# The second product of a feed-forward block turned over: features on partitions, residual and bias on VectorE, transposes after

## What is computed

```python
h = elu(_gat_heads(enc_inputs, adj, W_heads, a_heads))       # 4 heads, [B, N, 4*256]
out = elu(_gat_heads(h, adj, W_out[None], a_out[None])[:, 0]) # [B, N, 256]
ffn = jnp.maximum(out @ w1 + b1, 0.0) @ w2 + b2
y = ffn + out
mu, var = y.mean(-1, keepdims=True), y.var(-1, keepdims=True)
L1 = (y - mu) / jnp.sqrt(var + 1e-5) * ln_gamma + ln_beta
# the result is x1 + L1, with x1 the output of the first layer
```

## Time and profile before

| | |
|---|---|
| time, median of 3 runs | 1722.63 us (1721.34 to 1722.68) |
| span of the profiled execution | 1722.6 us |
| its own time beside the span | the same; nothing lies around the span |
| PE / weight loads busy | 1584.4 us (92%) / 1319.3 us (77%) |
| VectorE busy | 1452.3 us (84%) |
| ScalarE busy | 1382.1 us (80%) |
| GpSimd busy | 1004.7 us (58%) |
| mean granted clock of TensorE | 0.975 of full speed |

### The profile page before, as it was taken

The page is one execution under the profiler, slowest core; times in us unless marked ns, Lnnn a source line. Parts: engine busy times, 40 slices in busy tenths (PEclk is TensorE's granted clock), DMA queues, the critical chain, the costliest instruction groups (busy, mean ns, idle before and its releaser), DMA issues.

```text
span 1722.6 us, 36184 instructions
## 1 busy us (share of the span) xinstructions
PE 1584.4 (92%) x13119; PEld 1319.3 (77%) x13120; DVE 1452.3 (84%) x2520; ACT 1382.1 (80%) x1858; POOL 1004.7 (58%) x1425
## 2 busy tenths in 40 slices
PE   5548999999999999999999999999999999999965
PEld 3336878788787887788887887888777888888854
DVE  5877699879998899979999799988999798898583
ACT  4177499879988799878997799878997799999660
POOL 4064367447575566656575566656666475675271
PEclk9769999999999999999999999999999999999988
DMA  8266499749986698678977699868976698798572
GB/s 262 57 147 115 94 190 162 120 95 189 174 151 117 123 187 164 118 122 160 189 141 117 113 184 178 137 98 152 190 156 112 104 172 172 129 133 147 101 118 36
DMA packets 780882, 242.45 MB, mean 141 GB/s; under 512 B 746368, under 2 KB 774016, under 8 KB 780576
## 3 DMA queue, kind: packets, MB, share of 16 engines
q1 hardware_dynamic: 771744, 231.70, 72.1%
q0 software_dynamic: 8960, 8.42, 4.3%
HBM read 38.54 MB, written 16.94 MB: 32 GB/s over the span
## 4 chain that ended last, share of the span: by engine, by line
PE 49%; DVE 18%; ACT 13%; issue 10%; DMA 5%; POOL 3%; SPq 1%; DVEq 0%; ACTq 0%; POOLq 0%
PE ps L129 11%; PE ps L1260 7%; PE ps L1261 7%; PE ps L1266 7%; DVE p_lo L1041 5%; PE ps L138 5%; PE ps L1280 4%; PE ps L1293 3%; ACT p_hi L925 3%; ACT xr L912 3%; DVE xr L1034 3%; PE ps L1341 2%; DMA cat<-f_rows 2%; ACT xr L918 2%; DVE ht_lo L1066 2%
## 5 line engine op out<-in xcount | busy, mean ns | idle before, releaser
L1260 PE MATMUL ps<-pt_hi,hv_hi 128*128 128x256 f16 x2048 | 463.8, 274 | 26.4 <-DMA pt_hi<-p_hi 26.4
L1261 PE MATMUL ps<-pt_hi,hv_lo 128*128 128x256 f16 x2048 | 463.7, 274 | 0.0
L1041 DVE SCALAR_TENSOR_TENSOR p_lo<-xr,rden,p_hi 128x1024 f16<-128x1024 f32 x320 | 409.6, 1280 | 30.4 <-ACT p_hi L925 30.4
L925 ACT ACTIVATE p_hi<-xr,rden 128x1024 f16<-128x1024 f32 x320 | 365.4, 1142 | 32.8 <-POOL rden L849 32.8
L847 POOL TENSOR_SCALAR den<-sums 128x1 f32<-128x1 f32 x320 | 156.4, 489 | 363.2 <-ACT xr L918 361.2
L918 ACT ACTIVATE xr<-xr,shift 128x1024 f32<-128x1024 f32 x320 | 365.5, 1142 | 2.4 <-POOL shift L862 2.4
L1034 DVE CUSTOM_DVE_ANT_0 xr<-cat,mask_add 128x1024 f32<-128x1024 f32 x256 | 311.2, 1217 | 7.5 <-DMA cat<-f_rows 7.5
L912 ACT ACTIVATE xr<-xr,f1h 128x1024 f32<-128x1024 f32 x256 | 292.6, 1143 | 5.5 <-DVE mx L1034 5.5
L849 POOL TENSOR_TENSOR rden<-den,minus_one 128x1 f32<-128x1 f32 x320 | 268.3, 838 | 26.7
L860 POOL TENSOR_SCALAR zt<-mx,f1h 128x1 f32<-128x1 f32 x256 | 197.6, 772 | 120.0 <-DVE mx L1034 117.1
L1266 PE MATMUL ps<-pt_lo,hv_hi 128*128 128x256 f16 x2048 | 266.3, 273 | 0.9 <-DMA pt_lo<-p_lo 0.9
(11 more groups left out here) (192 smaller groups left out, 3193.3 us busy)
## 6 DMA issues: line engine op xcount, KB each, us to landing
cat<-f_rows SPq DMA_DIRECT2D x32, 512.0 KB, 4.6
out<-xx SPq DMA_DIRECT2D x32, 256.0 KB, 2.4
xx<-in_x SPq DMA_DIRECT2D x28, 256.0 KB, 3.3
out<-fin POOLq DMA_DIRECT2D x28, 256.0 KB, 5.3
pt_hi<-p_hi SPq DMA_TRANSPOSE x320, 3.3
pt_lo<-p_lo SPq DMA_TRANSPOSE x320, 3.3
adj_i<-in_adj SPq DMA_DIRECT2D x4, 1024.0 KB, 11.7
f2o<-f2o_rows SPq DMA_DIRECT2D x8, 512.0 KB, 4.4
```

Of the source, the lines that this page charges most:

```text
L925: nc.scalar.activation(p_hi[:, k % P_SLOTS, :], xr[:, k % X_SLOTS, :], ACT.Copy, scale=rden[:, k % 8:k % 8 + 1]).then_inc(hi_done, 1)
L1041: nc.vector.scalar_tensor_tensor(p_lo[:, k % P_SLOTS, :], xr[:, k % X_SLOTS, :], rden[:, k % 8:k % 8 + 1], p_hi[:, k % P_SLOTS, :], ALU.mu ...
L1260: nc.tensor.matmul(to, vh, hi, start=t == 0, stop=False)
L1261: nc.tensor.matmul(to, vl, hi, start=False, stop=False)
```

## The change

`ff2` now keeps features on partitions, like `ff1`: for each of two blocks of output features, w2 is the stationary operand and 512 tokens stream. The identity products are gone. `y_out` adds bias (a column now, `b2_col`) and residual on VectorE and writes into o2T in place. A new PE task, `turn_y`, turns the eight 128 by 128 blocks over with f32 transposes into psB. A new VectorE task, `norm_y`, takes stats and means from psB and does the gain from there, right away; only the gain (`lny_gain`) frees psB. The due steps of the FFN are set anew, and those of m0 to m3 with mj_high and mj_low (but not mj_low3) are one later in `STEADY`.

```diff
-        FFN = ("ff1_0", "ff2_0", "ff1_1", "ff2_1")
+        FFN = ("ff1_0", "ff2_0", "turn_y0", "ff1_1", "ff2_1", "turn_y1")
-        STEADY: m0=-31, m1=-30, m2=-29, m3=-28, mj_high0=-31, mj_high1=-29, mj_high2=-28, mj_high3=-27, mj_low0=-30, mj_low1=-29, mj_low2=-28, mj_low3=-25
+        STEADY: m0=-30, m1=-29, m2=-28, m3=-27, mj_high0=-30, mj_high1=-28, mj_high2=-27, mj_high3=-26, mj_low0=-29, mj_low1=-28, mj_low2=-27, mj_low3=-25
-        CLOSING = dict(ff1_0=-1, ff2_0=2, ff1_1=4, ff2_1=6, hidden_0=1, hidden_1=5, y_0=4, y_1=9, save_f2o=-22, load_f2o=-16)
-        LAST = dict(ff1_0=3, ff2_0=3, ff1_1=5, ff2_1=7, hidden_0=2, hidden_1=5, y_0=4, y_1=8, save_f2o=-13, load_f2o=-12)
+        CLOSING = dict(ff1_0=-1, hidden_0=0, ff2_0=1, y_0=2, turn_y0=3, norm_0=4, rstd_0=5, rescale_0=6, add_0=7,
+                       ff1_1=5, hidden_1=6, ff2_1=6, y_1=7, turn_y1=8, norm_1=9, rstd_1=10, rescale_1=11, add_1=12, save_f2o=-22, load_f2o=-16)
+        LAST = dict(ff1_0=3, hidden_0=3, ff2_0=3, y_0=4, turn_y0=4, norm_0=5, rstd_0=5, rescale_0=6, add_0=7,
+                    ff1_1=5, hidden_1=6, ff2_1=7, y_1=8, turn_y1=8, norm_1=9, rstd_1=9, rescale_1=10, add_1=11, save_f2o=-13, load_f2o=-12)
...
-            if name[:2] == "ff":
-                return (ff_done if name[:3] == "ff1" else y_done), 2 * s + i + 1
+            if name in FFN:
+                return {"ff1": ff_done, "ff2": y_done, "tur": lny_gain}[name[:3]], 2 * s + i + 1
...
             def y_out(p, i):
-                y = y_of(p, i).rearrange("p (t f) -> p t f", f=F)
-                nc.vector.tensor_tensor(y, general(which)[:, :].rearrange("p (t f) -> p t f", f=F), b2_bc[:, :].unsqueeze(1).to_broadcast([P, half, F]), ALU.add).then_inc(y_done, 1)
-                hold(dve, "dve", y_done, 2 * p + i + 1)
+                for m in range(KF):
+                    part = o2T_of(p, i)[:, m, :]
+                    last = nc.vector.scalar_tensor_tensor(part, general(which)[:, m * 512:(m + 1) * 512], b2_col[:, m:m + 1], part, ALU.add, ALU.add)
+                last.then_inc(y_done, 1)
+
+            def norm_y(p, i):
+                which, seq = bank(f"turn_y{i}", p)
+                dve.wait_ge(bank_full[which], seq + 1)
+                turned = general(which)[:, :].rearrange("p (t f) -> p t f", f=F)
+                if 2 * p + i:
+                    dve.wait_ge(lny_done, 2 * p + i)
                 for t in range(half):
-                    last = nc.vector.bn_stats(stats_y[:, t, :], y[:, t, :])
+                    last = nc.vector.bn_stats(stats_y[:, t, :], turned[:, t, :])
...
                 if 2 * p + i:
-                    hold(dve, "dve", lny_gain, 2 * p + i)
                     hold(dve, "dve", lny_pow, 2 * p + i)
...
-            def gain(p, i):
                 dve.wait_ge(lny_mv, 2 * p + i + 1)
                 for t in range(half):
-                    part = y_of(p, i)[:, t * F:(t + 1) * F]
-                    last = nc.vector.scalar_tensor_tensor(part, part, mv_y[:, t, 0:1], gamma_bc[:, :], ALU.subtract, ALU.mult)
+                    last = nc.vector.scalar_tensor_tensor(y_of(p, i)[:, t * F:(t + 1) * F], turned[:, t, :], mv_y[:, t, 0:1], gamma_bc[:, :], ALU.subtract, ALU.mult)
                 last.then_inc(lny_gain, 1)
...
             def ff2(p, i):
-                for t in range(half):
-                    tok = slice(t * P, (t + 1) * P)
-                    for k in range(KF):
-                        nc.tensor.matmul(to[:, t * F:(t + 1) * F], ff_half[:, k * 512 + t * P:k * 512 + (t + 1) * P], w2_sb[:, k, :], start=k == 0, stop=False)
-                    for k in range(KF):
-                        last = nc.tensor.matmul(to[:, t * F + k * P:t * F + (k + 1) * P], o2T_of(p, i)[:, k, tok], ident[:, :], start=False, stop=k == KF - 1)
+                for m in range(KF):
+                    last = product(to[:, m * 512:(m + 1) * 512], [(w2_sb[:, k, m * P:(m + 1) * P], ff_half[:, k * 512:(k + 1) * 512]) for k in range(KF)])
                 last.then_inc(full, 1)
+
+            def turn_y(p, i):
+                to, full = open_bank(f"turn_y{i}", p)
+                pe.wait_ge(y_done, 2 * p + i + 1)
+                for t in range(half):
+                    for k in range(KF):
+                        last = nc.tensor.transpose(to[:, t * F + k * P:t * F + (k + 1) * P], o2T_of(p, i)[:, k, t * P:(t + 1) * P], ident[:, :])
+                last.then_inc(full, 1)
```

More of the change, by code:

```diff
@@ L70, in build @@
         b1_col = sb("b1_col", [P, KF], F32)
-        b2_bc = sb("b2_bc", [P, F], F32)
+        b2_col = sb("b2_col", [P, KF], F32)
         gamma_bc = sb("gamma_bc", [P, F], F32)
@@ L251, in _ @@
                     sp.dma_start(ao_bc[:, :, :].rearrange("p c f -> p (c f)"), a_out.partition_broadcast(P)).then_inc(a_in, DMA)
-                    sp.dma_start(b2_bc[:, :], b2.partition_broadcast(P)).then_inc(c_in, DMA)
+                    sp.dma_start(b2_col[:, :], b2.rearrange("(k p) -> p k", p=P), allow_slow_non_contiguous=True).then_inc(c_in, DMA)
                     sp.dma_start(gamma_bc[:, :], gamma.partition_broadcast(P)).then_inc(c_in, DMA)
@@ L684, in build @@
         HEADS = ("rows", "f1T")
-        FFN = ("ff1_0", "ff2_0", "ff1_1", "ff2_1")
+        FFN = ("ff1_0", "ff2_0", "turn_y0", "ff1_1", "ff2_1", "turn_y1")
         STEADY = dict(load_x=-52, x_stats0=-47, x_stats1=-42, x_rstd=-40, x_norm0=-39, h0_high0=-39, h0_low0=-38, h0_high1=-37, h0_low1=-34,
-                      turn_h0_0=-38, turn_h0_1=-34, m0=-31, m1=-30, m2=-29, m3=-28, mj_high0=-31, mj_high1=-29, mj_high2=-28, mj_high3=-27,
-                      mj_low0=-30, mj_low1=-29, mj_low2=-28, mj_low3=-25, x1_00=-24, x1_01=-23, x1_10=-22, x1_11=-22, x1_out0=-22, x1_out1=-20,
+                      turn_h0_0=-38, turn_h0_1=-34, m0=-30, m1=-29, m2=-28, m3=-27, mj_high0=-30, mj_high1=-28, mj_high2=-27, mj_high3=-26,
+                      mj_low0=-29, mj_low1=-28, mj_low2=-27, mj_low3=-25, x1_00=-24, x1_01=-23, x1_10=-22, x1_11=-22, x1_out0=-22, x1_out1=-20,
                       save_x1=-21, x1_stats0=-22, x1_stats1=-17, x1_rstd=-16, x1_norm0=-15, hv_high0=-15, hv_low0=-14, x1_norm1=-14, hv_high1=-14,
@@ L892, in _ @@
                     for i in range(2):
-                        if due(n - 1, s, f"y_{i}"):
+                        if due(n, s, f"rstd_{i}"):
                             pool.wait_ge(lny_mv, 2 * s + i + 1)
@@ L896, in _ @@
                         for u in range(2):
-                            if due(n - 4 - u, s, f"y_{i}"):
+                            if due(n - u, s, f"add_{i}"):
                                 add_y(s, i, u)
@@ L1228, in _ @@
                             y_out(s, i)
-                        if due(n - 2, s, f"y_{i}"):
-                            gain(s, i)
-                        if due(n - 3, s, f"y_{i}"):
+                        if due(n, s, f"norm_{i}"):
+                            norm_y(s, i)
+                        if due(n, s, f"rescale_{i}"):
                             rescale(s, i)
@@ L1371, in _ @@
                             ff2(s, i)
+                        if due(n, s, f"turn_y{i}"):
+                            turn_y(s, i)
 _INS = ['x', 'adj', 'L0_gnn_W', 'L0_gnn_b', 'L1_gnn_W_heads', 'L1_gnn_a_heads', 'L1_gnn_W_out', 'L1_gnn_a_out',
```

## The result

The changed kernel takes 1765.8 us (median of 4 runs, 1761.25 to 1766.66), beside 1722.66 us for the kernel before on the same chip: a ratio of 1.0244, 95% interval 1.0229 to 1.0258. It is slower by 43 us in the medians. The forecast was slower, by 20.4 us: the direction was right, and the time lies outside the range of 1722 to 1756.

The account below looks back on a forecast made before the run. TensorE was taken to bound the time from ff1_0 to x1_1. Terms of 5.8 (ff1_1), 6.9 (m products), 1.0 and 1.5 (batch ends 5 and 6) and 5.2 (tail) sum to 20.4 us, so 1743 us, range 1722 to 1756.

Parts of the forecast that it names:

- The wait at ff1_1: Batch ends 0 to 4: TensorE starts ff1_1 1.85 us later, waiting for norm_0's gain; net +1.15 us each, 5.8 us.
- The m products: Moved one step later: two tight pairs per batch instead of one; +1.2 us five times, +0.9 in batch 2, 6.9 us.
- The clock after such waits: Rival: clock also falls after the 1.9 us waits at ff1_1, costing 1.8 us in five places; 1752 us, chance 0.08.
- Batch ends 5 and 6: Ends without front work (5) and with the bank wait in the open (6): +1.0 and +1.5 us.
- The tail: Last batch, nothing covers the longer chain: +3.4 us, plus 1.8 us for a lower clock; 5.2 us.
- Unit costs: Single operations in the FFN: ff2 product 3.44 us, eight transposes 1.1, norm_0 about 3.8, PSUM reads costing nothing more.
- the rival built on it: Rival: transposes take 0.275 us each, 1.1 us more at some seven batch ends; 1751 us, chance 0.05.
- bank free in time: Rival at ff1_1: neither hidden_0 nor norm_0 delays TensorE, so the kernel gets faster; 1718.8 us, chance 0.12.
- little change: Rival: TensorE's wait is half as long, m pairs cost what the old one did; 1722 to 1732 us, chance 0.15.

Follow-up runs that it names:

- the run of the m steps alone: The kernel before with only the change's new due steps for m0 to m3, mj_high and mj_low: 1734.22 us, ratio 1.0055.
- the run of the tail alone: The kernel before with the new path in batch 7 only, all m products as before: 1731.03 us, ratio 1.0026.
- both runs that tried it: Changed kernel with norm_0 one step earlier, 1764.71 us; changed kernel with rescale_1 at 12 and norm_0 split over steps 3 and 4, 1746.62 us.
- four idle operations: The kernel before with four unused VectorE operations between mj_low1 and its xx operations, in batches 2 to 7: 1739.62 us, ratio 1.0104.

## Why the prediction was off

The direction held, and so did the reading of the bound: time from ff1_0 to x1_1 is TensorE's, and the waits of the tally above came back in the total, as far as two profiled executions can be compared. Term by term, forecast and span to span:

- **The wait at ff1_1**, 5.8 us forecast. Waits of 1.94, 2.03, 2.22, 2.21 and 1.48 us, 9.9 in all for the 9.25 forecast, and a product at the low clock once, +1.7. A little low.
- **The m products**, 6.9 forecast: this is the step that failed. The prediction put VectorE "to mj_low0 at 1118.8" and ending at 1120.2, which left out rescale_1: it had moved from step 12 to 11, ahead of mj_low0, on the same engine. Counted from the start of ff1_1, it had TensorE ready for m1 after 33.3 us and VectorE at mj_low0 after 33.1; the trace has 33.3 and 32.9, and then the 1.67 us of rescale_1. The waits before m1 sum to 12.9 us for 6.0, so +6.9; four of the five took the clock down, +6.6; batch 2 cost 0.43 for 0.9. The term came to 20 us. With the 2.4 of ff1_1 the excess is some 15.4 us; up to the last x1 the trace shows 27.85 for the 12.7 forecast, 15.2 more. The run with rescale_1 at 12 took most of this back, 12.1 us up to there, and the run of the m steps alone gave 7.5 for the forecast's own 6.9.
- **The clock after such waits** was a rival with a chance of 0.08, argued down with the waits of 1.3 to 1.5 us in the tail. Those rows said nothing of 2 us and more; the rows above them, 2.90 and 9.11, spoke for the fall. It was right that the clock can fall behind such waits, and given too little chance. Its form, a fall after the wait at ff1_1, happened once in five there, but three times in five in the run with rescale_1 at 12.
- **Batch ends 5 and 6**, 1.0 and 1.5 forecast, 1.9 and 3.6 measured. In batch 6 ff1_1 starts 4.2 us later behind ff1_0 than before (3.9 forecast), and up to the last batch's ff1_0 only 0.6 of it is regained where 2.4 was assumed.
- **The tail**, 5.2 forecast, 3.5 in the trace, 4.5 by the run of the tail alone. The longer chain in half 0 is 3.4 us as worked out; the clock cost 1.4, not 1.8; and half 1 saved 1.3 us where it had been given 0.3: from ff1_1 to the end 25.9 us, 1.4 of it the clock, for 25.8 before.
- **Unit costs** held: ff2_0 3.51 us up to the next pair, eight transposes 0.93, norm_0 3.7, statistics from PSUM 1.41 for four. The Trainium skill ("TensorE: Matmul & The Clock Gate", Part 4) has 275 ns for a transpose; in a row of eight the trace has 0.93 us, 0.12 each, so the rival built on it is out.

The rivals "bank free in time" and "little change" are out too: each would need a wait under 1 us at ff1_1, and it was 1.5 to 2.2. What stays open is when a wait of 2 to 3 us takes the clock down and when it does not; and why the version with six batches on the new path, whose batch 6 and tail are the old ones, loses another 6.8 us behind the last x1 in its trace, though the run of the tail alone loses 3.3 between the last x1 and its last ff2_0 with nothing changed there.

## What to carry to other kernels

When steps are renumbered, write out the new order on each engine and look for everything that now stands ahead of an operation that frees a shared bank; here 1.67 us of rescale that nobody waited for cost 11 to 17 us. What stands ahead matters only where that engine is late: 1.66 us of gain in the same place cost nothing in the kernel before with the new m steps, where VectorE had 1.22 us to spare. For a wait of TensorE of some 2 us or more, reckon with a slow product behind it in some of the places, and give both sums. And where the engine that is waited for has no idle time in the stretch, moving its work about moved the wait and hardly shortened it, in both runs that tried it.

## What the runs showed of the hardware

- The granted clock can fall to 0.50 after shorter pauses than the 2.90 us seen before, but need not. Waits up to 1.85 us before FFN and m products left these at full length in all twelve traces, from 300 us on. From 1.92 to 2.25 us it went both ways: 2.03 and 2.21 were followed by 3.70 us in the changed kernel, 2.03, 2.04 and 2.21 by 5.40 with rescale_1 moved. From 2.45 to 2.90 us eight of fifteen m products in three kernels were slow: three of four in the changed kernel, five of six with four idle operations, none of five with norm_0 a step earlier. From 3.05 to 3.76 us it was five of six. So the length of the wait alone does not decide. Up to 2.90 us a fall costs an m product 1.4 to 1.7 us, and an ff1 1.7.
- Eight f32 transposes of 128 by 128 take 0.93 us up to the next matmul at full clock (granted clock 1.00) and 1.94 at half (batch 6 of the changed kernel, 0.50). Among attends the clock stayed at 1.00 through them.
- BATCH_NORM_STATS2 from PSUM takes 1.41 us for four, and the gain from PSUM 1.66, no more than the 1.69 from SBUF.
